# Attention scores of two heads on two halves of the TensorE array, with the attention steps of a chunk spread over half steps

## The reference, cut to what matters

```python
# x: (64, 128, 256)   ctx: (64, 128, 192)   16 heads of 64, all f32
q = xn @ Wq + lora(xn);  k, v = ctx[:, :124] @ Wk, Wv + lora;  ki, vi = ctx[:, 124:] @ Wk_ipa, Wv_ipa
out = softmax(q k^T / 8) v + softmax(q ki^T / 8) vi        # two softmaxes: 124 and 4 context rows
x = x + out @ Wo + bo + lora(out)
# then x = x + FFN(layernorm(x)): quantised 256 -> 1024, a 3-tap convolution over tokens, silu, quantised 1024 -> 256
```

## Time and profile before

| | us |
|---|---|
| three runs | 1666.96, 1671.57, 1673.72 (median 1671.57) |
| profiled execution, its own time | 1673.32 |
| its span, first to last instruction | 1671.2 |
| busy in the span: PE, weight loads, DVE, ACT, POOL | 1474.9, 1168.1, 1305.2, 1183.1, 729.1 |
| mean granted TensorE clock | 0.967 of full |

### The profile page before, as it was taken

How to read it: one execution, slowest core, us unless ns; L and a number is a source line. 1 busy time by engine, 2 the same in 40 slices (tenths; PEclk the granted TensorE clock), 3 DMA queues, 4 the chain that set the end, 5 groups by cost and what they waited for, 6 DMA issues and landing times.

```text
span 1671.2 us, 33198 instructions
## 1 busy us (share of the span) xinstructions
PE 1474.9 (88%) x10586; PEld 1168.1 (70%) x10586; DVE 1305.2 (78%) x3157; ACT 1183.1 (71%) x3925; POOL 729.1 (44%) x1085
## 2 busy tenths in 40 slices
PE   7999999989899998989899998989999898988642
PEld 3688777777777777777777777777777777776521
DVE  4264798888878798787879888887878878787876
ACT  2477776868677786968778686867778696876521
POOL 0144445444544444444444544454444445444400
PEclk9899999999999999999999999999999999999855
DMA  7300001000000100000010100000010000000000
GB/s 187 117 28 15 28 15 42 15 25 15 26 27 13 40 13 27 13 26 27 13 40 13 40 10 27 17 26 27 13 40 13 27 13 26 27 1 26 1 13 13
DMA packets 41129, 47.14 MB, mean 28 GB/s; under 512 B 3008, under 2 KB 35200, under 8 KB 41088
## 3 DMA queue, kind: packets, MB, share of 16 engines
q1 hardware_dynamic: 40032, 45.82, 8.9%
q10 hardware_dynamic: 1056, 0.81, 0.2%
HBM read 36.13 MB, written 10.49 MB: 28 GB/s over the span
## 4 chain that ended last, share of the span: by engine, by line
PE 35%; DVE 32%; ACT 20%; issue 11%; DMA 0%; POOL 0%; DVEq 0%; ACTq 0%; POOLq 0%
ACT SM L644 8%; DVE GBS L876 7%; PE PS L460 6%; PE PS L422 4%; PE PS L517 4%; PE PS L403 4%; PE PS L438 4%; PE PS L447 3%; PE PS L412 3%; PE PS L473 3%; DVE GBS L887 2%; ACT H L669 2%; DVE GBS L866 2%; ACT GBS L674 2%; DVE H L894 2%
## 5 line engine op out<-in xcount | busy, mean ns | idle before, releaser
L1029 POOL TENSOR_TENSOR SM<-SM,RC 128x496 f32<-128x496 f32 (+1 forms) x512 | 340.3, 686 | 730.5 <-DVE RC L802 730.5
L644 ACT ACTIVATE SM<-PS,MX 128x124 f32<-128x124 f32 x1024 | 359.3, 365 | 200.1 <-DVE SM L808 197.1
L460 PE MATMUL PS<-KT,QM 128*128 128x128 f32 x2048 | 279.2, 279 | 26.3 <-ACT SM L644 26.2
L460 PEld LDWEIGHTS PS<-KT,QM 128*128 128x128 f32 x2048 | 249.4, 192 | 42.7 <-ACT SM L644 41.5
L1061 POOL TENSOR_TENSOR OTl<-OF,OTh 128x256 fp32r<-128x256 f32 x256 | 216.4, 846 | 5.6 <-ACT OF L638 5.6
L644 ACT ACTIVATION_READ_ACCUMULATOR SM<-PS,MX 128x1 f32 x1024 | 211.0, 206 | 0.0
L447 PE MATMUL PS<-IDF,SM 128*128 128x128 f32 x1024 | 169.3, 288 | 18.9 <-POOL SM L1029 18.8
L636 ACT ACTIVATE OTh<-PS 128x256 fp32r<-128x256 f32 x256 | 99.6, 389 | 103.2 <-PE PS L438 99.4
L438 PE MATMUL PS<-PT,V 128*64 128x128 f32 x2048 | 170.2, 288 | 0.0
L806 DVE TENSOR_REDUCE MX<-PS 128x4 f32<-128x496 f32 x256 | 169.9, 664 | 0.0
L438 PEld LDWEIGHTS PS<-PT,V 128*64 128x64 f32 x2048 | 107.8, 137 | 83.5 <-issue 77.0
(11 more groups left out here) (142 smaller groups left out, 3693.8 us busy)
## 6 DMA issues: line engine op xcount, KB each, us to landing
XIN<-in_x SPq DMA_DIRECT2D x16, 512.0 KB, 3.6
XRES<-in_x SPq DMA_DIRECT2D x16, 512.0 KB, 3.5
out_y<-H SPq DMA_DIRECT2D x16, 512.0 KB, 3.0
CRAW<-in_ctxT SPq DMA_DIRECT2D x16, 256.0 KB, 2.8
RRAW<-in_ctxT SPq DMA_DIRECT2D x32, 128.0 KB, 2.8
QM<-in_Wq SPq DMA_DIRECT2D x1, 1024.0 KB, 11.0
GBS<-in_Wo SPq DMA_DIRECT2D x1, 1024.0 KB, 21.6
k_ipa_columns<-H SPq DMA_DIRECT2D x1, 1024.0 KB, 5.1
```

Source lines behind the costliest of these rows:

```text
L460: m = mm(psS[:, h, :], QM[:, 2 * q + h // 2, h % 2, TOK * b:TOK * b + TOK], KT[:, 2 * q + h // 2, b, :], start=True, stop=True)
L644: m = act.activation(SM[s % 2][:, h, 0:ORG], psS[:, h, 0:ORG], ACT.Exp, bias=MX[s % 2][:, h:h + 1], accum_out=SU[s % 2][:, h:h + 1])
L1029: m = pool.tensor_tensor(part, part, RC[c % 2][:, 4 * i:4 * i + 4].unsqueeze(2).broadcast_to(shape), ALU.mult)
```

## The change

Six things are done together.

1. Q is stored once: `QT` [128, 8, 512], one copy on ACT per tile in place of two. The two POOL memsets and the semaphore `zeroed` go. The raw weights land in `QT` and in a new tile `STAGE` of the freed size.
2. Each score matmul runs over 64 array rows: heads 0 and 2 of the quad on rows 0 to 63, heads 1 and 3 on rows 64 to 127, issued in turn 0, 1, 2, 3. The first pair of rows writes PSUM bank 0, the second bank 1. The order of heads in `SM`, `MX`, `SU` and `PT` becomes 0, 2, 1, 3.
3. `psT` moves to bank 2, over `psO`. The wait for `ot_high` (the output copies of the chunk before) moves from `p_v` to `transpose_p`.
4. PE: even half steps have `p_v` and `project_out`; odd ones `transpose_p` and `scores`.
5. ACT: even half steps begin with `output_copies` and then the exponentials of heads 2 and 3 and of the extra rows for chunk s-1; odd ones begin with `transposed_copy` and end with the exponentials of heads 0 and 1 of chunk s.
6. DVE does sums and maxima in odd half steps, POOL normalises in odd and makes the low part in even ones.

```diff
-        QM = sb("QM", [P, PAIRS, 2, T])
+        QT = sb("QT", [P, PAIRS, T])
+        STAGE = sb("STAGE", [P, 4096])
...
-        psS = PS[:, 0, :].rearrange("p (h k) -> p h k", h=4)
-        psT = PS[:, 1, :].rearrange("p (h k) -> p h k", h=4)
+        psS = PS[:, 0:2, 0:2 * TOK].rearrange("p r (a k) -> p r a k", a=2)
+        psT = PS[:, 2, :].rearrange("p (h k) -> p h k", h=4)
         psO = PS[:, 2, 0:2 * TOK].rearrange("p (a k) -> p a k", a=2)
...
                     pe.wait_ge(pt_done, gc.count(CHUNKS, c + 1))
-                    need(pe, ot_high, gc.count(CHUNKS, c))
...
-                               PT[:, h, :], start=True, stop=True)
+                               PT[:, 2 * (h % 2) + h // 2, :], start=True, stop=True)
...
                     pe.wait_ge(p_done, gc.count(CHUNKS, c + 1))
+                    need(pe, ot_high, gc.count(CHUNKS, c))
                     for h in range(4):
                         m = pe.transpose(psT[:, h, :], SM[c % 2][:, h, :], IDF[:])
...
-                        m = mm(psS[:, h, :], QM[:, 2 * q + h // 2, h % 2, TOK * b:TOK * b + TOK],
-                               KT[:, 2 * q + h // 2, b, :], start=True, stop=True)
+                        rows = slice(DH * (h % 2), DH * (h % 2) + DH)
+                        m = mm(psS[:, h % 2, h // 2, :], QT[rows, 2 * q + h // 2, TOK * b:TOK * b + TOK],
+                               KT[rows, 2 * q + h // 2, b, :], start=True, stop=True)
...
             def steps(g, n):
                 if n % 2 == 0:
                     p_v(g, n // 2)
+                    project_out(g, n // 2)
+                else:
                     transpose_p(g, n // 2)
                     scores(g, n // 2)
-                    project_out(g, n // 2)
...
-                        act.activation(QM[0:64, 2 * q + a, 0, :], psU[u % 2][0:64, :], ACT.Identity)
-                        act.activation(QM[64:128, 2 * q + a, 1, :], psU[u % 2][64:128, :], ACT.Identity).then_inc(unit_free[u % 2], 1)
+                        act.activation(QT[:, 2 * q + a, :], psU[u % 2], ACT.Identity).then_inc(unit_free[u % 2], 1)
...
-            def exponentials(g, s):
+            def exponentials(g, s, heads):
                 if g.exists():
-                    act.wait_ge(sub_done, g.count(CHUNKS, s + 1))
-                    for h in range(4):
+                    if heads[0] == 0:
+                        act.wait_ge(sub_done, g.count(CHUNKS, s + 1))
+                    for h in heads:
...
+                    if heads[-1] < 3:
+                        return
                     m.then_inc(s_used, 1)
...
                 if n % 2 == 0:
                     output_copies(g, n // 2)
+                    gc, c = chunk_at(g, n // 2 - 1)
+                    exponentials(gc, c, (2, 3))
+                else:
                     transposed_copy(g, n // 2)
...
-                if n % 2 == 0:
-                    exponentials(g, n // 2)
+                if n % 2 == 1:
+                    exponentials(g, n // 2, (0, 1))
...
-                if n % 2 == 0:
-                    attend(g, n // 2)
+                if n % 2 == 1:
+                    sums(g, n // 2)
+                    maxima(g, n // 2)
...
-                if half == 0 and gc.exists():
+                if half == 1 and gc.exists():
                     pool.wait_ge(rec_done, gc.count(CHUNKS, c + 1))
...
-                if half == 1 and gc.exists():
+                if half == 0 and gc.exists():
                     pool.wait_ge(ot_high, gc.count(CHUNKS, c + 1))
```

## The result

The changed kernel takes **1821.78 us** (1818.68 to 1823.2, 4 runs) against 1671.41 for the kernel before, measured beside it: a ratio of 1.090 [1.089, 1.092]. It is 150 us slower where 64 us less was forecast. The profiled execution has a span of 1816.8 us.

A forecast was written before the change was run, and what follows sets the result against it. No engine was full: PE was busiest at 88%, DVE close behind, the chain changing engine all the time. From 1673.3, scores 17, Q copy 28 and half steps 20 came off: 1608, median 1607 us, range 1560 to 1685.

The forecast's parts named there:

- half steps: `p_v` and `project_out` leave the scores' half step on PE, shortening DVE's and ACT's waits; 20 us gain, between 0 and 62.
- The wait that is moved: With psT over psO, PE's transposes wait for ACT's output copies and `p_v` for PT; costed at nothing.
- I count on no fall: PE's clock in the loop stays up, with PE busy about 90% of a shorter group.
- The bank, as a rival: Bank 2 locks PE and ACT together at `p_v`'s wait for the PT copy; 90 us more, 1697; chance 0.14.
- locked: Sign of the bank rival in the trace: PE waits over 60 us in total for ACT's PT or output copies.
- Scores: Score matmuls on two row halves on PE save 0.15 us a chunk in 113 chunks; 17 us gain, bounds gain 51, loss 34.
- pairs with two switches: Score row halves run in overlapping pairs plus a mode switch in and out: 0.74 us a chunk, from 0.89.
- no overlap: Rival: score row halves run one after another on PE, 1.19 us a chunk; 1659, or up to 1679; chance 0.11.
- the second half of the rule: On PE, a weight load may overlap running matmuls when the row group differs; no run had shown it.
- The Q copy: One Q copy on ACT instead of two gives back 0.59 us per pair on the chain; 28 us gain, bounds 0 and 76.
- a saving counts in the share in which its line is on the chain: Rule used to size terms: a line's saving counts for its share of the chain of what ended last, no more.
- DVE takes over: Rival: DVE's 79.65 us of work a group doesn't shrink and half of each gain is swallowed; 1639; chance 0.13.

The follow-up runs named there:

- order_own: Kernel before with only the new half-step order (items 4 to 6); padded scores, two Q copies and psT's own bank stay; 1856.98 us, ratio 1.113.
- one_half_step: Changed kernel's row halves, single Q copy and shared bank in the old half steps, scores and `project_out` between `p_v` and transposes, four SM buffers; 1812.31 us, 1.085.
- own_ffn_shift: order_own with the whole feed-forward schedule one half step later, projections unmoved; 1853.91 us, ratio 1.110.
- flip_own: order_own with even and odd half steps exchanged for the attention; 1787.31 us, ratio 1.070.
- flip_own_nosplit: flip_own with all four exponentials at the end of the even half step; 1767.06 us, ratio 1.058.
- halves_late_pv: halves_in_row with `p_v`, `project_out` and output copies in the odd half step behind the even one used before, PT with two buffers; 1820.29 us, 1.089.
- after_filler: Changed kernel with 20 unused matmuls a group ahead of two PE stops (8 and 12); 1782.09 us, ratio 1.067.
- order_shared: order_own plus the shared bank (item 3), the output-copy wait at the transposes; 1859.05 us, ratio 1.114.
- before_shared: Kernel before, in its old order, with psT over psO in bank 2; 1917.05 us in a single run.
- one_half_step_late: one_half_step with ACT's PT copy moved behind the unit and feed-forward copies, ahead of the exponentials; 1670.61 us, ratio 1.000.
- halves_in_row: Kernel before, order kept, with unpadded Q, one copy, and score row halves one behind the other in one bank, a wait between; 1778.76 us, 1.064.
- before_one_copy: Kernel before with one 128-partition Q copy per unit on ACT instead of two, zero rows not kept; 1669.04 us, ratio 0.998.

## Why the prediction was wrong

**The step that failed** is "half steps", booked as a gain of 20 us between 0 and 62. It is a loss of 188 us (order_own). I asked only what the scores would no longer stand behind on PE, and not what ACT and DVE would find at the head of their queues. "The wait that is moved" was costed at nothing "because ACT is now 4.7 us a group less busy", and only PE's waits and what is behind them were named. Of the waits of PE, ACT and DVE the one that grew most is ACT's, for the transposes: 0.7 to 202.3 us. In the kernel before, the PT copy stands behind two output copies, and the transposes are over by then; in the new order it is the first thing in ACT's odd half step, while PE is just coming to them. Busy time that ACT no longer has is no cover for an ACT that stands in its queue.

How much of the 188 that one wait makes is not shown. The pair one_half_step shows that it can cost 142 us by itself; own_ffn_shift, with 117 us of the same wait, took as long as order_own with 168, so it is not the only one. What is shown of the 188: about 70 go back when scores, maxima and exponentials return to even half steps (flip_own); 98 stay where `p_v`, `project_out` and output copies are parted from the transposes (flip_own_nosplit). The hand-over over PT was ruled out only where the same move costs 22 us (halves_late_pv). About 40 of the change's 150, across all of this, go with PE's clock (after_filler). No run moved the PT copy alone in the kernel after, and what stays of the 98 without ACT's waits is open.

**The clock.** "I count on no fall" was wrong: I argued from PE's mean share, and the fall came behind two stops of a group, of 2.24 and 3.43 us in the windows above, which the mean doesn't show. Why it didn't come behind stops of 2.22 and 2.67 us is open.

**The bank, as a rival.** I named bank 2 as the slower way with a chance of 0.14 and a time of 1697, its place the wait of `p_v` for PT. That wait measured 26.7 us, the transposes' wait for the output copies 51.9; sharing costs 2 us in the new order. By my own mark, over 60 us of PE's waits in total, the trace would have read "locked", and order_shared says that it isn't: a wait that is long in a trace is not a price until it is taken away. The mechanism is right for the old order (248 us in before_shared).

**Scores.** The guess of pairs with two switches, 0.74, was on the safe side. By the measure that it was made with, pieces of the chain, the kernel after has 0.65 in place of 0.89:

```profile
1045.85 0.44 PE PS L447 x4
1046.28 0.65 PE PS L461 x8
```

That saves 0.24 a chunk, not 0.15; the records span 0.71 us in place of 1.05 to 1.16, and the scores' busy time is 87 us less. The first line bears out the working too: four transposes that don't follow `p_v` take the 0.44 that it gave them (in one_half_step_late, behind `project_out`, they do so too), and the 0.59 of the earlier trace rows behind `p_v` has the 0.15 of the switch. The rival "no overlap" is false. The weight loads of the scores after, by line and then in one chunk:

```profile
L461 PEld LDWEIGHTS PS<-KT,QT 64*128 64x128 f32 x2048 | 141.7, 196 | 49.4 <-issue 35.9 <-ACT SM L645 13.4
```

```profile
1062.57 0.52 PEld L461 LDWEIGHTS PS<-KT,QT 64*128 64x128 f32 x8 [0.17 <-issue]
1062.57 0.71 PE L461 MATMUL PS<-KT,QT 64*128 64x128 f32 x8
```

One load takes 196 ns, near the 192 of the earlier trace rows, but eight are done in 0.52 us. Four loads of one row half alone take 0.52 as well, as the line of halves_in_row at 1019.61 shows. So loads of the two row groups run beside each other and beside matmuls. The trace now agrees with the second half of the rule that the prediction took from the Trainium skill, "TensorE: Matmul & The Clock Gate", Part 2.

**The Q copy** was mis-sized: 3 us in place of 28. I took each pair on the chain as worth its 0.59 us; the waits of before_one_copy show that the next wait took it back, the maxima or `p_v`. The bound "0, if another wait ends there first" was near the truth. In the new order it can be otherwise: scores and copies, forecast at 17 + 28 = 45, bring 37 there together (order_shared against the kernel after), and how they share it was not tried.

**Together**, one_half_step_late has both gains in the old half steps and stands at 1.000: PE is busy 68 us less than in the earlier trace rows, and the time is the same. Its own order is not free either: ACT waits 136.8 us for the transposes, and PE 25.5 us for PT. So what the gains would bring without any such wait is not shown, but "a saving counts in the share in which its line is on the chain" was too hopeful for this kernel. The chain of one_half_step_late, shares by engine and by line:

```profile
PE 39%; DVE 37%; ACT 12%; issue 10%; DMA 0%; POOL 0%; DVEq 0%; ACTq 0%; POOLq 0%
DVE GBS L880 7%; PE PS L474 6%; PE PS L461 5%; PE PS L422 5%; PE PS L403 5%; ACT SM L644 4%; PE PS L412 4%; PE PS L518 4%; PE PS L447 3%; PE PS L437 3%; DVE GBS L870 3%; DVE H L861 3%; DVE H L875 2%; DVE MX L810 2%; DVE H L855 2%
```

DVE has nearly as much of the chain as PE, with the feed-forward reduce (L880 here) first; before, it was PE 35%, DVE 32% and ACT 20%. That reads like the rival "DVE takes over", at 1671 where I priced it at 1639; it is argued from the chain and was not tested.

## What to carry to other kernels

Before a step moves to another place of an in-order queue, ask for each engine what it will wait for at the head of that place, how far the producer is by then, and what stands behind the wait: in one_half_step the same copy cost 142 us more in one place of ACT's queue than in another. But don't take the length of a wait for its price: 117 and 168 us of the same wait stood in kernels of the same time. In a pipeline of engines that are each 70 to 88% busy, take a term read from shares of the chain with zero as a serious value; here 73 us of copies gave 2 to 3. Test the order and the savings as separate kernels.

## What the runs showed of the hardware

Matmuls of half height on the two halves of the array's rows run side by side, here into two banks: eight f32 records of 64x128 in 0.71 us, where one half behind the other's end takes 1.47 and eight of full height 1.05. Their weight loads do so too: eight in 0.52 us, as long as four of one half alone. The granted clock fell to its lower level behind stops of PE of 2.24 and 3.43 us and stayed up behind others of 2.22 and 2.67, so the length of a stop alone doesn't tell. Filling such stops can pay: 20 useless matmuls a group raised the mean clock from 0.927 to 0.968 and took 40 us off. Two engines that pass one bank back and forth directly, once in each of 256 chunks, paid 248 us for it in the one run of before_shared.
